# A two-layer graph kernel on one core: the second norm in halves, joined query and key weights, and a new order of the tiles' work in both diffusion steps

## The reference

```python
def _L0_gnn_ref(input_features, adj, W, b):
    A = (adj != 0).astype(input_features.dtype)
    hidden = input_features @ W + b
    deg = jnp.sum(A, axis=0)
    return A @ hidden / deg[:, None]

def _adj_from_feats(Xa, W1, W2, W3):
    Q = Xa @ W1
    K = Xa @ W3
    logits = Q @ W2 @ K.T / TAU
    # sort each row, keep the largest until their softmax sums to P_NUC = 0.9
    ...
    masked = jnp.where(keep, logits, -jnp.inf)
    return jax.nn.softmax(masked, axis=1)

def _L1_gnn_ref(X, S, W1, W2, W3, U1, U2, U3, gamma, beta):
    S = S + jnp.eye(n, dtype=X.dtype)
    Rf = S / jnp.clip(S.sum(axis=1, keepdims=True), 1e-12)
    Rb = S / jnp.clip(S.sum(axis=0), 1e-12)[:, None]
    Xf, Xb, Xa = (X, X, X)
    for s in range(STEPS):                      # STEPS = 2
        A = _adj_from_feats(Xa, W1, W2, W3)
        Xf = Rf @ Xf
        Xb = Rb @ Xb
        Xa = A @ Xa
        Z = Z + (Xf @ U1[s] + Xb @ U2[s] + Xa @ U3[s])
    Y = X + Z
    ...                                         # layer norm of Y, times gamma, plus beta

h = jnp.maximum(_layernorm(x, axis=-1), 0.0)
x = x + _L0_gnn_ref(h, adj, L0_gnn_W, L0_gnn_b)
h = jnp.maximum(_layernorm(x, axis=-1), 0.0)
x = x + _L1_gnn_ref(h, adj, ...)
```

## Time and profile before

| | us |
|---|---|
| median of 3 runs (lowest to highest) | 2332.01 (2331.26 to 2335.74) |
| profiled execution | 2333.33 |
| its span | 2331.6 |
| PE busy | 1941.1 (83%) |
| DVE busy | 1935.2 (83%) |
| ACT busy | 1690.1 (72%) |
| POOL busy | 803.0 (34%) |
| mean granted TensorE clock, of full speed | 0.952 |

### The profile page before, as it was taken

How to read it: one execution, slowest core, us unless ns; L and a number is a source line. 1 busy time by engine, 2 the same in 40 slices (tenths; PEclk the granted TensorE clock), 3 DMA queues, 4 the chain that set the end, 5 groups by cost and what they waited for, 6 DMA issues and landing times. The chain is left out here.

```text
span 2331.6 us, 32861 instructions
## 1 busy us (share of the span) xinstructions
PE 1941.1 (83%) x10002; PEld 1254.8 (54%) x10002; DVE 1935.2 (83%) x6082; ACT 1690.1 (72%) x1754; POOL 803.0 (34%) x1386
## 2 busy tenths in 40 slices
PE   2999853999999999999883788898898988888883
PEld 1555421666666666666661555555565656555652
DVE  6777666888888888888747799999999999999985
ACT  4434236788888888888825888888888898889830
POOL 2000042244444444444424333333343434343403
PEclk9999976999999999999996899999999999999997
DMA  6777321111111111101115001010101010101023
GB/s 224 283 283 287 132 84 37 42 52 38 42 52 52 52 50 51 52 33 48 49 53 200 19 21 42 21 42 21 42 21 42 21 42 21 42 21 41 20 67 133
DMA packets 65725, 167.61 MB, mean 72 GB/s; under 512 B 7037, under 2 KB 45307, under 8 KB 61947
## 3 DMA queue, kind: packets, MB, share of 16 engines
q1 hardware_dynamic: 65530, 165.43, 20.4%
...
## 5 line engine op out<-in xcount | busy, mean ns | idle before, releaser
L1329 PE MATMUL banks<-xa,pt 128*128 128x256 f32 x2704 | 636.2, 387 | 41.4 <-ACT pt L906 41.4
L1329 PEld LDWEIGHTS banks<-xa,pt 128*128 128x128 f32 x2704 | 500.3, 191 | 184.4 <-issue 69.8
L882 ACT ACTIVATE junk_a<-pb_all,minus_t 128x3327 f16<-128x3327 f32 x151 | 464.2, 3074 | 167.2 <-POOLq L811 164.7
L1373 PE MATMUL banks<-region,at 128*128 128x512 f16 x2028 | 471.3, 394 | 0.0
L887 ACT ACTIVATE junk_a<-pb_all,minus_t 128x3327 f16<-128x3327 f32 x151 | 463.6, 3070 | 2.6
L796 POOL TENSOR_SCALAR over<-over,points 128x1 f32<-128x1 f32 x151 | 136.4, 904 | 769.4 <-ACT junk_a L887 769.3
L1373 PEld LDWEIGHTS banks<-region,at 128*128 128x128 f16 x2028 | 204.5, 101 | 247.0 <-issue 33.9
L1294 PE MATMUL banks<-keys,qs 64*128 64x512 f32 (+1 forms) x832 | 205.4, 584 | 114.7 <-DVE pb_all L1183 52.8
L906 ACT ACTIVATE pt<-banks 128x896 f32<-128x896 f32 x208 | 173.3, 861 | 108.0 <-PE banks L1321 108.0
L1183 DVE TENSOR_SCALAR_CACHE_REDUCE pb_all<-banks 128x1024 f32<-128x1024 f32 x260 | 209.1, 848 | 25.9 <-PE banks L1294 22.7
L1052 DVE MAX8 junk_v<-below 128x8 f32<-128x208 f32 (+1 forms) x624 | 222.2, 429 | 2.2
...
## 6 DMA issues: line engine op xcount, KB each, us to landing
...
```

What stands on the lines that cost most here:

```text
L882: nc.scalar.activation(junk_a[:, 0:w], pb[u][:, 0:w], ACT.Relu, scale=sign, bias=t, accum_out=over[u][:, 0:1])\
L1329: last = nc.tensor.matmul(bank[4][:, 0:D], pt[sl][:, t * P:(t + 1) * P], xa[:, t0 + t, :], start=(t0 + t == 0), stop=(t0 + t == T - 1))
L1373: last = nc.tensor.matmul(bank[5][:, :], at[i.slot][:, t, :], mov, start=(n == 0 and t == 0), stop=(n == PARTS - 1 and t == T - 1))
```

## The change

- The second norm is done in two halves of 13 tiles. The degree arithmetic (`degrees`) and the residual and statistics of the first 6 tiles (`AHEAD`) move into the last tiles of the adjacency block on DVE. ACT's second square root stands before the last group of the first half. The waited all-reduce is used after both halves.
- The query and key weights stand side by side in `wqk_sb` (128 columns), so that one pair of products makes both, in the second block and in step 0.
- The queries of tiles 0 and 1 are loaded for step 0 in the second block, and for step 1 during step 0. ACT ends the second block with an exponential of one column.
- Tile 0 of step 0 has no ACT levels: DVE does all four bisections.
- In step 0, ACT does both sums of a level together (`STEPS`), copies queries and keys after the fourth copy, and copies the own rows after the last sums. PE turns the own rows (`turn_own`) behind the sums, and does the last two products by U and the joined weights (`rest_of_z`) one tile later, between the second transposes and the first product. DVE adds z later in the search and masks before it waits for the flag count.
- At the end of step 0 PE makes the logits of step 1's tile 0 (`logits_ahead`), DVE takes them, ACT takes the exponential and DVE does its three coarse levels (`coarse_search`). Step 1's tile 0 then has no levels on ACT and POOL.
- In step 1, PE turns the own rows between the two halves of the sums and counts the flags in the middle of the second half. POOL does the first fine level ahead of adding z.

The diff, cut to its core:

```diff
-    FIRST_BISECTIONS = (1, 0)
-    LEVELS = [[r + f] + [r + a] * (T - 1) for r, f, a in zip(ROUGH, FIRST_BISECTIONS, ACT_BISECTIONS)]
+    FIRST_BISECTIONS = (0, 0)
+    LEVELS = [[r + f if r == 0 else 0] + [r + a] * (T - 1) for r, f, a in zip(ROUGH, FIRST_BISECTIONS, ACT_BISECTIONS)]
...
-    wq_sb = sb("wq_sb", [P, KD, DA], f32)
-    w3_sb = sb("w3_sb", [P, KD, DA], f32)
+    wqk_sb = sb("wqk_sb", [P, KD, 2 * DA], f32)
...
+    AHEAD = 6
+
+    def degrees(dve):
...
+    def residuals(dve, t0, t1):
+
+        dve.wait_ge(sem("hw_done"), t1)
+        for t in range(t0, t1):
+            nc.vector.scalar_tensor_tensor(out=x_all[:, t, :], in0=xa[:, t, :], scalar=rdeg[:, t, :],
+                                           in1=x_all[:, t, :], op0=ALU.mult, op1=ALU.add).then_inc(sem("x1"), 1)
+        for t in range(t0, t1):
+            dve.wait_ge(sem("x1"), t + 1)
+            nc.vector.bn_stats(stats[:, t, :], x_all[:, t, :]).then_inc(sem("ln_stats"), 1)
+
+    def row_stats(dve, t0, t1):
+
+        dve.wait_ge(sem("ln_stats"), T + t1)
+        for t in range(t0, t1):
+            nc.vector.bn_aggr(mv[:, t, :], stats[:, t, :]).then_inc(sem("ln_mv"), 1)
+        dve.wait_ge(sem("ln_mv"), T + t1)
...
+                if i.static and i.t == T - 2:
+                    degrees(dve)
+                    residuals(dve, 0, AHEAD)
...
+                if g == 2:
+                    sp.wait_ge(sem2("q_stored")[0], 16)
+                    for m in range(2):
+                        for h in range(2):
+                            sp.dma_start(qs[m][h * DA:(h + 1) * DA, :], q_d[0, m]).then_inc(sem2("step_q_loaded")[m], 16)
...
+            residuals(dve, AHEAD, HT)
+            row_stats(dve, 0, HT)
+            layernorm_scalars(dve, 1, 1.0, 0, HT)
+            residuals(dve, HT, T)
+            row_stats(dve, HT, T)
+            layernorm_scalars(dve, 2, 1.0, HT, T)
             dve.wait_ge(sem("ratio_all"), 1)
+            ch = Chain(dve, "kappa_chain")
...
+                if t0 + n == HT:
+                    layernorm_sqrt(act, 2, HT, T)
+                if t0 == HT:
+                    act.wait_ge(sem("ln_ready"), 3)
+            nc.scalar.activation(over[0][:, 6:7], ident[:, 0:1], ACT.Exp)
...
+                for c in range(KD):
+                    last = nc.tensor.matmul(bank[4 + g % 2][:, 0:n * P], wqk_sb[:, c, :], xT[g % 2][:, c, 0:n * P],
+                                            start=(c == 0), stop=(c == KD - 1))
...
+                        if first and T <= m.t < T + 2:
+                            after(sp, "negmax", m + -1)
+                            sp.wait_ge(S("qo_stored"), 16 * 2)
+                            for h in range(2):
+                                sp.dma_start(qs[m.slot][h * DA:(h + 1) * DA, :], q_d[1, m.t - T]).then_inc(S2("q_loaded")[m.slot], 16)
+                        if m.inside(T) and m.t >= 2:
...
+                    if not first:
+                        level(j, EARLY)
+                        if (i + -2).inside(T):
+                            add_z(i + -2)
...
                         level(j, e)
                     if not first:
...
-                STEPS = ((), (0,), (1,), (2, 3), (4,), (5,)) if first else ((), (4, 5), (6, 7), (8, 9), (), (11,))
+                STEPS = ((), (0, 1), (), (2, 3), (), (4, 5)) if first else ((), (4, 5), (6, 7), (8, 9), (), (11,))
...
-                        if first and c == 1 and (k + -1).inside(T):
+                        if first and c == NT - 1 and (k + -1).inside(T):
                             queries_keys(k + -1)
...
+                        if not first:
+                            own_turned(k)
                     if j.inside(T):
                         for n in STEPS[NT + 1]:
                             sums(j, n)
+                    if first and k.inside(T):
+                        own_turned(k)
+                    if first and i.t == T + 1:
+                        exponentials(nxt)
...
+                    tg = targets[i.third][:, :]
+                    if first and i.t == 0:
+                        dve.wait_ge(S("exp"), i.n + 1)
+                        Chain(dve, "step_goal").link(nc.vector.tensor_scalar(tg, ms[:, 0:1], NUCLEUS, None, ALU.mult))
+                        dve.sem_inc(S("p_ready"), 1)
...
-                        add_z(i + -2)
...
                     take_logits(i + 2, 0, 2)
+                    if first:
+                        add_z(i + -2)
                     pool_of = cand
...
                         ch.link(nc.vector.tensor_tensor(unsettled[:, :], none[:, :], flaw[:, :], ALU.max), hold=True)
                     dve.sem_inc(S("unsettled"), 1)
                     if first:
+                        ch.add(nc.vector.scalar_tensor_tensor(out=p, in0=p, scalar=left_max[:, :], in1=p, op0=ALU.is_gt, op1=ALU.mult))
...
 
+                def coarse_search(j):
+
+                    ch = Chain(dve, "step_coarse")
+                    p, t, lim = pb[j.third][:, 0:WSUB], rough_t[j.third], over[j.third][:, 5:6]
+                    dve.wait_ge(S("exp"), j.n + 1)
+                    nc.vector.tensor_scalar(targets[j.third][:, :], mass[j.third][:, 0:1], NUCLEUS, None, ALU.mult)
+                    ch.link(nc.vector.tensor_scalar(lim, mass[j.third][:, 0:1], (1.0 - NUCLEUS) * WSUB / N, None, ALU.mult))
+                    for e in range(ROUGH[1]):
+                        up, down = math.exp(MOVES[1][e]), math.exp(-MOVES[1][e])
+                        to = t[:, e + 1:e + 2] if e < ROUGH[1] - 1 else thr[j.third][:, 2:3]
+                        ch.link(nc.vector.scalar_tensor_tensor(out=below[:, 0:WSUB], in0=p, scalar=t[:, e:e + 1], in1=p,
+                                                               op0=ALU.is_lt, op1=ALU.mult, accum_out=below_sum[:, :]))
+                        ch.link(nc.vector.tensor_scalar(factor[:, :], below_sum[:, :], lim, up - down, ALU.is_le, ALU.mult))
+                        ch.link(nc.vector.scalar_tensor_tensor(out=to, in0=factor[:, :], scalar=down, in1=t[:, e:e + 1],
+                                                               op0=ALU.add, op1=ALU.mult))
+                    dve.sem_inc(S("p_ready"), 1)
+
                 def body(i):
...
                     else:
-                        take_logits(i + 2, 0, NL)
+                        if first or i.t > -2:
+                            take_logits(i + 2, 0, NL)
                         spread(i + -1)
                         add_z(i + -2)
+                        if first and i.t == T:
+                            take_logits(nxt, 0, 3)
+                        if first and i.t == T + 1:
+                            take_logits(nxt, 3, NL)
+                            coarse_search(nxt)
                     if not first and i.static and i.t == T - 1:
                         for u in range(2):
                             dve.wait_ge(S2("y_done")[u], T - 1)
...
+                def logits_ahead(c):
+
+                    last, (c0, w) = Idx(0, T - 1, 0, 6), LCH[c]
+                    pe.wait_ge(S2("q_loaded")[nxt.slot], 32 * (nxt.use + 1))
+                    pe.wait_ge(S("qk_done"), T if c == len(LCH) - 1 else T - 1)
+                    pe.wait_ge(S("logits_free"), NL * T + max(0, c - 1))
...
+                    for h in range(2):
+                        r = slice(h * DA, (h + 1) * DA)
+                        nc.tensor.matmul(pt_ps[c % 2][:, h * CW:h * CW + w], qs[nxt.slot][r, :], keys[r, HW + c0:HW + c0 + w],
+                                         start=True, stop=True).then_inc(S("logits_psum"), 1)
...
+                def rest_of_z(k):
+
+                    pe.wait_ge(S("xoT"), k.n + 1)
+                    last = times_u(4, 6)
+                    if first:
+                        for c in range(KD):
+                            last = nc.tensor.matmul(bank[7][:, D:D + P], wqk_sb[:, c, :], zt[:, 4 + c, :], start=(c == 0), stop=(c == KD - 1))
+                    last.then_inc(S("z_psum"), 1)
...
                             if c + 1 < NT:
                                 transposes(c + 1)
+                            if first and c == 0 and (k + -1).inside(T):
+                                rest_of_z(k + -1)
                             if c >= 2 and m.inside(T):
                                 logits(m, c - 2, c - 1)
+                            if first and i.t == T and c >= 2:
+                                logits_ahead(c - 2)
                             product(c)
-                    if m.inside(T):
+                    if first and i.t == T:
+                        logits_ahead(2)
+                    if m.inside(T) and (first or m.t > 0):
                         logits(m, 2 if k.inside(T) else 0, len(LCH))
...
+                        if not first and not i.inside(T):
+                            turn_own(k)
...
+                            if n == 1 and k.inside(T):
+                                turn_own(k)
                             for t in range(T):
```

(13 more changed lines are left out.)

118 lines of the change are left out of this document (48 added, 70 removed).

## The result

| | before | after |
|---|---|---|
| median | 2332.38 us (4 runs, 2331.26 to 2335.74) | 2220.27 us (4 runs, 2217.95 to 2222.13) |
| ratio | | 0.9516 (95% 0.9502 to 0.953) |
| span of the profiled execution | 2331.6 us | 2218.3 us |
| busy PE / DVE / ACT / POOL | 1941.1 / 1935.2 / 1690.1 / 803.0 us | 1896.4 / 1940.6 / 1683.4 / 665.4 us |

What follows compares the result with a forecast made beforehand. No engine is full; each tile is a ring of hand-overs, with idle stretches outside the tiles. Terms 33 + 24.5 + 3.3 + 9.9 + 4.5 + 1.5 + 11.5 + 6.4 = 94.6 us off 2333.3 gave 2238, range 2219 to 2263.

Steps and rivals of the forecast that it cites:

- step (d): Step 0, regular tiles: DVE's mask (3.7 us) ahead of the answer covers the 2.5 us flag wait; alone gains nothing.
- The ring that it closed: Step 0 tile: chain of ACT and PE hand-overs from ACT's first transposes' copy, 27.0 us work plus 2.7 waits, period 29.7.
- R1: Step 0: PE and ACT wait for each other oftener, period near 30.7, 22 us less gain, 2260 us; chance 0.22.
- R2: Step 0: PE becomes the bound at 28.9 and the norm is undisturbed, 18 + 3 us more, 2217; chance 0.10.
- POOL's level ahead of its z sum costs nothing: Step 1: POOL's level moved ahead of adding z is free, as POOL idles there; no gain counted.
- 10 x 0.97 and one more: Step 1: alternating 38.7 and 39.7 us tiles all become 38.73; 10 tiles gain 0.97, one more before, 11.5 us in all.
- 24.5 + 3.3: Second norm gains 24.5 us (bounds 19 and 27.5); queries loaded before the barrier bring step 0's first logits 3.3 sooner.
- If nothing disturbs: Second norm's end: step 0 begins at about 326.5 against 353.7 without disturbance; 329 taken, for slower DVE adds beside POOL's scaling.
- 8.6 + 0.9 + 2.2: Second norm: further DVE work for the second half after the first, at about 295; ready at 307.6 or later.
- (c) and (d): End of step 0: own rows turned behind the sums and mask before the answer; tile 25's cut at +29.2, not +32.9.
- R3: Step 1: PE starts each tile at a lowered clock after resting; the 11.5 us gain vanishes or becomes 3 loss, 2251; chance 0.10.
- R4: Step 1: PE at half clock for most of each tile, slower than before, 2382 at 10 us lost per tile; chance 0.02.

Runs made afterwards that it cites:

- the first try: Changed kernel with the queries of step 1's tile 2 loaded at the head of step 1, ahead of the bulk loads: 2225.37 us, ratio 0.9544.

## Why the prediction was right, point by point

The direction and the range held; the time came out 18 us below the forecast, 1.3 us inside the range's lower end, and that for reasons of which two were not those given. Step 1 alone gave 17.9 us more than its term (29.4 for 11.5), and all other terms together 0.9 more than theirs: step 0's tiles 5.3 more, the others 4.4 less.

- **Step 0, regular tiles.** Forecast 29.7, measured 29.48. The signs came: no flag wait, none at the first product, and the wait for the level 1.4 us, not the 2 to 3 forecast. But step (d) failed, "Alone it would gain nothing": alone it gives 1.27 of the 1.74 us. The prediction had both facts in hand, the 1.56 us of POOL's instruction beside the mask and the mask's move, and used the saving only inside the new ring; in the old one it went unpriced. The orders, to which it gave the gain, add 0.47 us together with the joined weights. The ring that it closed runs over TensorE's transposes of f and b and leaves out the one of the table above, over VectorE's cut and search, POOL's levels and ScalarE's sums. In the changed kernel the two are equally long: in the tile cut at 656.64 POOL's level is ready at 670.12, ScalarE's copy of the transposes ends at 670.20, and its next sum starts at 670.21. So 29.7 was right for the new kernel, and wrong was what set the old period. R1 (30.7) did not come, R2's 28.9 neither: TensorE is busy 28.2 of 29.48 us.
- **Step 1.** This is the term that was mis-sized: 11.5 predicted, 29.4 measured over all of it. The forecast period of 38.73 is what the kernel has with the flag wait gone and POOL's order old, within 0.2 (38.56 measured). The failed step is "POOL's level ahead of its z sum costs nothing": it gains 0.52 us a tile. The earlier trace rows show the cut at 3.68 in step 0 and at 4.21 in step 1, the same instruction on the same shapes; the difference was not asked about. The tiles up to the fourth cut give 5.3 us more, for which the sum had only one tile's 0.97. (Its own 10 x 0.97 and one more make 10.7, not 11.5.)
- **Second norm.** First logits 26.5 us sooner against 24.5 + 3.3. ScalarE's first norm came at 294.56 (295 forecast), the second half's scalars at 307.04 (307.6), the step's first logits at 330.77 (329). "If nothing disturbs" failed at one place: POOL's first scaling could begin at 295 and began at 299.56, as the last of VectorE's 13 additions of 0.40 us (294.44 to 299.66) ended. It came 5.0 us behind ScalarE's first norm; in the kernel before and with the norm whole, where no additions stand there, it came 0.7 us behind. VectorE was not slowed (5.22/13 = 0.40), while the term had reckoned with a slower VectorE. POOL's scalings then ended at 326.9 and not past 328. The second half's terms 8.6 + 0.9 + 2.2 behind 295 make 306.7, not the 307.6 written; 13 additions and 13 statistics are 9.5, not 8.6.

Behind these misses stands one behaviour. In the kernel before 151 of POOL's instructions start inside a VectorE pass over 3327 columns with two SBUF inputs (more than 0.3 us ahead of its end), in the changed kernel 104, and none of them ends before the pass: 1.56 and 3.75 us for instructions of 0.26 and 0.28. The other way, the cut is longer by 0.53 us when POOL's addition begins with it.

The Trainium skill (SBUF — State Buffer, "Who interferes with whom") says that a vector instruction with two SBUF inputs contends with a GpSimd one that reads SBUF, and that the ports they share are an exclusive lock. The traces here agree. The prediction set the rule aside because L606's median did not show it; the level's 1.56 us and the 4.21 us of the cut did.

- **First tiles of step 0.** 4.8 us against 6.8 from cut 0 to cut 2. The mask alone, on the kernel before, brings this stretch from 63.58 to 58.85; in the changed kernel it is 58.75, and 60.75 with the mask behind. So the mask's place alone gives the whole of it, and with the mask ahead the other edits add nothing visible here. (In the forecast of the first cut, 12.6 + 4 x 4.17 - 0.4 + 2.25 make 31.1, not 31.4.)
- **End of step 0 and change of step.** 4.9 against 6.0. Tile 25's cut follows tile 24's by 32.6, not 29.2, as "(c) and (d)" had it; with the mask behind it is 29.2, and the time is lost further on instead. Tile 2's queries are awaited still (32.2 us), and the cut they delay is tile 1's, 43.1 us after tile 0's. What the wait is worth by itself is not shown: the first try took it away, but brought a collision with it and was slower.
- **Tile 24 of step 1.** 5.9 against 6.4.
- **R3, R4, the clock.** Granted clock 0.97 in step 1's regular part against 0.98: no loss seen, neither rival came.

What stays open: which step of the forecast for cut 0 to 2 of step 0 was 2 us too high, what each part of the second norm besides the halves gives, and the 0.2 us between the forecast 38.73 and the 38.56 of step 1 with POOL's old order.
